# Routing dense edges by half-width column tiles instead of full-width blocks

## The reference

```
h   = relu(layernorm(x))
msg = relu([h[dst], edge_attr] @ W1a + b1a) @ W1b + b1b      # per edge
summed, counts = segment_sum(msg, src), segment_sum(1, src)  # per node
agg = summed / max(counts, 1)
out = x + relu([h, agg] @ W2a + b2a) @ W2b + b2b
```

## Time and profile before

| | |
|---|---|
| median of 2 runs | 1411.84 us (1411.36 to 1412.31) |
| span of the profiled execution, first to last instruction | 1414.2 us |
| mean granted TensorE clock | 0.978 of full speed |
| instructions | 66554, of which TensorE 27554 matmuls and as many weight loads |

### The profile page before, as it was taken

One profiled execution on the slowest core, in us unless ns is written; L12 is line 12 of the kernel. 1 busy time (PEld: TensorE's weight loads), 2 busy tenths in 40 slices (PEclk: granted clock), 3 DMA queues, 4 the chain that ended last, 5 costly groups with the idle time before them and its releaser, 6 DMA issues. The chain is left out here.

```text
span 1414.2 us, 66554 instructions
## 1 busy us (share of the span) xinstructions
PE 1339.5 (95%) x27554; PEld 1298.9 (92%) x27554; DVE 1341.4 (95%) x4186; ACT 869.4 (61%) x1857; POOL 1106.0 (78%) x732
## 2 busy tenths in 40 slices
PE   4667999999999999999999999999999999999967
PEld 3556999999999999999999999999999999999965
DVE  7889999999999999999999999999999999999886
ACT  6246666666666666666666666666666666666505
POOL 3538888888888888887888878888788887888753
PEclk8779999999999999999999999999999999999988
DMA  4767767767777777776777767776677876777451
GB/s 153 303 145 142 120 116 124 123 116 128 125 123 128 116 124 122 123 128 122 119 121 130 129 112 121 127 128 127 108 122 128 125 134 101 125 126 123 64 154 48
DMA packets 225080, 178.60 MB, mean 126 GB/s; under 512 B 149632, under 2 KB 191742, under 8 KB 223751
## 3 DMA queue, kind: packets, MB, share of 16 engines
q1 hardware_dynamic: 130468, 145.66, 39.7%
q0 software_dynamic: 94304, 28.63, 28.5%
HBM read 140.88 MB, written 33.31 MB: 123 GB/s over the span
## 5 line engine op out<-in xcount | busy, mean ns | idle before, releaser
L651 POOL DMA_INDIRECT sums<-vv,sidx x648 | 1043.8, 1611 | 249.9 <-issue 185.7
L892 ACT ACTIVATE area<-rank_ps 64x392 bf16<-64x392 f32 x1150 | 563.7, 490 | 138.1 <-PE rank_ps L1589 114.0
L1603 PE MATMUL rank_ps<-area 128*128 128x65 bf16 x17250 | 614.6, 193 | 1.6 <-issue 1.6
L1603 PEld LDWEIGHTS rank_ps<-area 128*128 128x128 bf16 x17250 | 593.8, 98 | 11.0 <-issue 2.0
L1589 PE MATMUL rank_ps<-r_d,oh 128*128 128x196 bf16 x4600 | 497.6, 250 | 13.3 <-DVE oh L1154 5.3
L1589 PEld LDWEIGHTS rank_ps<-r_d,oh 128*128 128x128 bf16 x4600 | 381.5, 97 | 27.1 <-issue 7.7
L1169 DVE TENSOR_SCALAR area<-iota,local 128x640 bf16<-128x640 int16 x1150 | 397.4, 410 | 4.1
L1154 DVE TENSOR_SCALAR oh<-iota,rank 128x640 bf16<-128x640 int16 x920 | 312.3, 409 | 4.8 <-PE rank_ps L1589 3.7
L869 ACT ACTIVATE r_d<-z_ps 128x512 f32<-128x512 f32 x247 | 147.5, 597 | 81.5 <-PE z_ps L1559 77.9
L880 ACT ACTIVATE vv<-c_ps 128x396 f32<-128x396 f32 x108 | 54.1, 501 | 175.7 <-PE c_ps L1578 165.2
L1553 PE MATMUL z_ps<-wts,et_d 128*128 128x128 f32 x920 | 131.9, 287 | 1.1 <-ACT r_d L869 0.7
(11 more groups left out here) (203 smaller groups left out, 794.8 us busy)
## 6 DMA issues: line engine op xcount, KB each, us to landing
ids_s<-ids SPq DMA_DIRECT2D x216, 192.0 KB
et_d<-in_e_t SPq DMA_DIRECT2D x115, 256.0 KB
ids_d<-ids SPq DMA_DIRECT2D x115, 256.0 KB
et_s<-in_e_t SPq DMA_DIRECT2D x108, 192.0 KB
sums<-vv,sidx POOLq DMA_INDIRECT x648
sums<-dense POOLq DMA_DIRECT2D x4, 1657.5 KB
wp_s<-p_table SPq DMA_DIRECT2D x216, 15.8 KB
wp_d<-p_table SPq DMA_DIRECT2D x115, 15.8 KB
```

The lines of the kernel that those rows point to most:

```text
L651: nc.gpsimd.indirect_dma_start(out=sums[t][:, :], out_offset=bass.IndirectOffsetOnAxis(ap=index, axis=0), in_=rows, in_offset=None, comput ...
L892: ins = nc.scalar.activation(routed[on, t.div(MACRO).mod(2), first:second + 1:second - first, t.mod(MACRO), :], bank[on, :, :], ACT.Copy)
L1603: ins = nc.tensor.matmul(l2_ps[h][:, u * W:u * W + w], oh2[:, g, u * P:(u + 1) * P], rows[:, PARTS[r]:PARTS[r] + w], start=g % MACRO == 0 ...
```

## The change

A routing matmul now takes weights that are 64 wide: the places of one bucket alone. For each bucket the four tiles of the first side write the lower 64 partitions of the bank, and the four tiles of the other side the upper 64, by turns. A fill is two buckets, and a bank holds both halves of each, so one activation copies it whole. The swap of buckets on the second side, and with it five of GpSimd's six operations on `place`, is gone. The branch that doesn't run here gets an index per half, a transfer and some small operations more. Other hunks rename a constant.

```diff
-FILLS = (((0, 0), (0, 1)), ((0, 2), (0, 3)), ((1, 0), (0, 4)), ((1, 1), (1, 2)), ((1, 3), (1, 4)))
+FILLS = tuple((b, b + 1) for b in range(0, BUCKETS, 2))
...
-                halfway = [slice(k * SUB * DENSE, (k + 1) * SUB * DENSE) for k in range(SIDES)]
-                nc.gpsimd.tensor_scalar(place[:, halfway[1]], bucket_b[:, halfway[1]], 0.5, -0.25, ALU.mult, ALU.add).then_inc(place_step, 1)
...
+                nc.gpsimd.tensor_scalar(place, bucket_b, float(PLACES), 1.0, ALU.mult, ALU.add).then_inc(place_step, 1)
...
                         bank = l1_ps[f % 2][:, 0:2 * RW].rearrange("p (i c) -> p i c", c=RW)
+                        first, last = FILLS[f]
                         if fit:
-                            for half in range(SIDES):
-                                first, second = (bucket_at(side, block, half) for side, block in FILLS[f])
-                                on = slice(half * PLACES, (half + 1) * PLACES)
-                                ins = nc.scalar.activation(
-                                    routed[on, t.div(MACRO).mod(2), first:second + 1:second - first, t.mod(MACRO), :], bank[on, :, :], ACT.Copy)
-                            ins.then_inc(routed_ready, 1)
+                            nc.scalar.activation(routed[:, t.div(MACRO).mod(2), first:last + 1, t.mod(MACRO), :], bank,
+                                                 ACT.Copy).then_inc(routed_ready, 1)
                             return
...
-                    for i, (side, block) in enumerate(FILLS[f]):
-                        for k in range(side * SUB, (side + 1) * SUB):
-                            ins = nc.tensor.matmul(l1_ps[f % 2][:, i * RW:(i + 1) * RW], oh1[:, k, block * P:(block + 1) * P],
-                                                   halves(DN, t)[:, k, :], start=k == side * SUB, stop=k == (side + 1) * SUB - 1)
+                    for i, bucket in enumerate(FILLS[f]):
+                        for k in range(SUB):
+                            for side in range(SIDES):
+                                strip = slice(side * PLACES, (side + 1) * PLACES)
+                                ins = nc.tensor.matmul(l1_ps[f % 2][strip, i * RW:(i + 1) * RW],
+                                                       oh1[:, side * SUB + k, bucket * PLACES:(bucket + 1) * PLACES],
+                                                       halves(DN, t)[:, side * SUB + k, :], start=k == 0, stop=k == SUB - 1)
                     ins.then_inc(routing, 1)
```

More of the change, by code:

```diff
@@ L22 @@
 ROWE = GE[DN] + GE[S]
-ROWG = 1 + SIDES
+WINDOWS_S = 2
+ROWG = 1 + WINDOWS_S
 BUCKETS = 10
@@ L104, in done @@
     return n + START
-def bucket_at(side, block, half):
-    return 2 * block + (half ^ side)
 def cols(m, n):
@@ L147, in cycles, with gnn_kernel @@
         s = s.plus(n)
-def gnn_kernel(nc, x, e_t, e_rows, src_col, dst_col, src_row, dst_row, weights, row_biases, out):
+def gnn_kernel(nc, x, e_t, e_rows, src_col, dst_col, src_strips, src_row, dst_row, weights, row_biases, out):
     f32, i32, i16, bf16 = mybir.dt.float32, mybir.dt.int32, mybir.dt.int16, mybir.dt.bfloat16
@@ L280, in gnn_kernel @@
         src_td = spare[:, TILES[DN] * RW + GE[DN] // 2:TILES[DN] * RW + GE[DN] // 2 + DT]
-        assert TILES[DN] * RW + GE[DN] // 2 + DT <= NTP * D and COLS <= 5 * 2 * HALF
+        strip_limit = spare[:, TILES[DN] * RW + GE[DN] // 2 + DT:TILES[DN] * RW + GE[DN] // 2 + DT + STRIPS]
+        assert TILES[DN] * RW + GE[DN] // 2 + DT + STRIPS <= NTP * D and COLS <= 5 * 2 * HALF
         near = rank[:, 0:(2 * ROWS_S + ROWS_D) * 3 * D // 2].bitcast(bf16).rearrange("p (k c d) -> p k c d", c=3, d=D)
@@ L765, in cycle @@
                         if routes:
-                            pool.wait_ge(dsidx_ready, done(t.value(1)))
-                            scatter_any(DN, landed(s.base + n, routed_groups), dsidx[:], lambda k: dsame[:, k, 0:W])
+                            pool.wait_ge(dsidx_ready, done(t.times(STRIPS, STRIPS)))
+                            for strip in range(STRIPS):
+                                scatter_any(DN, landed(s.base + n, routed_groups) + strip * TILES[DN] // ANY_TABLES, dsidx[:, strip, :],
+                                            lambda k: dsame[:, k, 0:W])
                             for at in range(ANY_TABLES):
@@ L887, in keep_routed @@
                         bank = l1_ps[f % 2][:, 0:2 * RW].rearrange("p (i c) -> p i c", c=RW)
+                        first, last = FILLS[f]
                         if fit:
-                            for half in range(SIDES):
-                                first, second = (bucket_at(side, block, half) for side, block in FILLS[f])
-                                on = slice(half * PLACES, (half + 1) * PLACES)
-                                ins = nc.scalar.activation(
-                                    routed[on, t.div(MACRO).mod(2), first:second + 1:second - first, t.mod(MACRO), :], bank[on, :, :], ACT.Copy)
-                            ins.then_inc(routed_ready, 1)
+                            nc.scalar.activation(routed[:, t.div(MACRO).mod(2), first:last + 1, t.mod(MACRO), :], bank,
+                                                 ACT.Copy).then_inc(routed_ready, 1)
                             return
-                        tiles = [side * SUB + block for side, block in FILLS[f] if block < SUB]
                         if f == 0:
                             act.wait_ge(dense_ended, done(t.value()))
-                        if not tiles:
+                        if last >= TILES[DN]:
                             act.wait_ge(routed_ready, done(t.times(len(FILLS), f)))
@@ L902, in keep_routed @@
                             return
-                        nc.scalar.activation(dsame[:, tiles[0]:tiles[-1] + 1, :], bank[:, 0:len(tiles), :], ACT.Copy).then_inc(routed_ready, 1)
+                        nc.scalar.activation(dsame[:, first:last + 1, :], bank, ACT.Copy).then_inc(routed_ready, 1)
                     def cycle(s, n, t, routes, sums_too):
@@ L1366, in dense_rows @@
                             dve.wait_ge(dsum_ready, done(t.times(2, r)))
[L1367 to L1371, removed]
+                        sources = src_td[:, column_of(DN, t):column_of(DN, t) + TILES[DN]]
+                        for j in range(STRIPS):
+                            nc.vector.scalar_tensor_tensor(out=dpick[:, j::STRIPS], in0=dsame[:, j::STRIPS, W],
+                                                           scalar=strip_limit[:, j:j + 1], in1=sources[:, j::STRIPS], op0=ALU.is_lt,
+                                                           op1=ALU.mult).then_inc(dpick_ready, 1)
+                        dve.wait_ge(dpick_ready, done(t.times(STRIPS, STRIPS)))
+                        for strip in range(STRIPS):
+                            on = slice(strip * PLACES, (strip + 1) * PLACES)
+                            nc.vector.tensor_scalar(dsidx[on, strip, :], dpick[on, :], trash[on, 0:1], None, ALU.add).then_inc(dsidx_ready, 1)
                     def cycle(s, n, t, routes, sums_too):
@@ L1408, in general @@
                     dve.wait_ge(ptab_out, 16 * len(P_PARTS))
-                    step(nc.vector.tensor_scalar(src_td, srcf[:, 0:DT], untrash[:, 0:1], None, ALU.add))
+                    dve.wait_ge(dst_in, 32)
+                    step(nc.vector.tensor_scalar(src_td, src_td.bitcast(i32), untrash[:, 0:1], None, ALU.add))
+                    for strip in range(STRIPS):
+                        on = slice(strip * PLACES, (strip + 1) * PLACES)
+                        for j in range(STRIPS):
+                            step(nc.vector.tensor_scalar(strip_limit[on, j:j + 1], limit[on, 0:1], 2.0 ** (PLACES * (strip - j)), None,
+                                                         ALU.mult))
                     step(nc.vector.memset(basew[:], -1.0))
                     step(nc.vector.memset(oh1[:], 0.0))
-                    dve.wait_ge(place_step, 6)
+                    step(nc.vector.memset(dpick[:], 0.0))
+                    for strip in range(STRIPS):
+                        step(nc.vector.tensor_scalar(dsidx[:, strip, :], dpick[:], trash[:, 0:1], None, ALU.add))
+                    dve.wait_ge(place_step, 1)
                     step(nc.vector.memset(words(0, n_routed + n_oh2), 0.0))
@@ L1527, in _ @@
                         pe.wait_ge(ranks_kept, b - 1)
-                    for side, bank in enumerate((l2_ps[b % 2], l1_ps[b % 2])):
-                        mine = masks[:, b, side * SUB:(side + 1) * SUB, :]
-                        ranks = bank[:, 0:SUB * DENSE].rearrange("p (k g) -> p k g", k=SUB)
+                    for half, bank in enumerate((l2_ps[b % 2], l1_ps[b % 2])):
+                        mine = masks[:, b, half * HALF_TILES:(half + 1) * HALF_TILES, :]
+                        ranks = bank[:, 0:HALF_TILES * DENSE].rearrange("p (k g) -> p k g", k=HALF_TILES)
                         for r in range(TURNS):
@@ L1536, in _ @@
                         for before in range(1, SUB):
```

(6 more changed lines are left out.)

36 lines of the change are left out of this document (14 added, 22 removed).

## The result

The changed kernel takes 1533.48 us (two runs, 1532.85 to 1534.11) against 1411.84 before: 1.0866 times as long, 95% interval 1.0835 to 1.0898, or 121.6 us more. The forecast was 1515 us, +104.

What follows compares the result with a forecast made beforehand. TensorE was taken to bound the kernel. Copies, routing pairs, weight loads and GpSimd's place step at 0 and changes of width at +104 us, added to the median of 1411.84, gave 1515 us; range 1404 to 1703, with 82% in it.

Steps and rivals of the forecast that it cites:

- The bound: Main loop: TensorE leads, VectorE has 2.1% of slack, ScalarE 35%; ScalarE follows and its saved copy work is worth nothing.
- Pairs: Routing on TensorE: two 64-wide matmuls run side by side at 87.5 ns, as one full-width matmul did; cost 0.
- Rival 2: Routing pairs: the halves run one after the other, +402 us and somewhat more with the changes, from 1814 us; chance 14%.
- Weight loads: Routing on TensorE: two 64-wide loads take at most 60.6 ns, hidden under the pair's 87.5 ns; cost 0.
- The 104 us kept for them: Routing weight loads falling back to the fp32 pace: 22.5 ns more a pair over 4600 pairs, kept for the range.
- Changes of width: TensorE entering and leaving half-width routing blocks: 1150 changes at 0.09 us, +104 us; bounds 0 and 187 us.
- Rival 1: TensorE routing: pairs side by side, loads hidden, changes free; 1404 to 1420 us, centre 1412; chance 32%.
- Rival 3: Block edges on TensorE: each change waits the whole recorded tail, 1599 us, or 1703 with loads at fp32 pace; chance 12%.
- Rival 4: Routing pairs: half-width matmuls stream quicker, a pair under 81.4 ns, over 2% faster, down to 1378 us; chance 4%.
- ScalarE's 8 us: TensorE's waits for ScalarE's copies, 1.7 + 6.0 us, mostly in the first five cycles: bound -8 us, taken as 0.

Runs made afterwards that it cites:

- the two copying experiments: Kernel before with one 128-partition copy per bank in place of two of 64: 1411.92 us; changed kernel with two 64-partition copies per bank: 1533.36 us.
- one strip: Changed kernel with the matmuls of both sides writing the lower 64 partitions, the upper ones left out: 1921.96 us, one run.
- The small matmuls in the kernel before: Kernel before with one extra 16-column matmul between the two accumulations of every fill: half-width 1537.25 us, full-width 1425.80 us.
- the joined kernel above: Kernel before with fp32 matmuls of the next scattered and next dense group issued next to each other, bf16 ones behind: 1407.80 us, ratio 0.9966.

## Why the prediction was right

- **The bound.** TensorE leads, ScalarE is off the path: shown by the two copying experiments, 1.0007 and no difference.
- **Pairs.** Taken at 87.5 ns with the halves side by side; measured 88.8 ns, and in one strip twice that. The speedup that the Trainium skill's "TensorE: Matmul & The Clock Gate", "Measured speedup vs the span model", gives for column tiles agrees in kind: two tiles took hardly longer here than one full-width matmul. Rival 2, the halves in turn, is the one-strip kernel at 1922 us.
- **Weight loads.** Taken as hidden: inside a block they are, at 88.8 ns a pair, although a 64-wide load is recorded with 108 ns and a 128-wide one with 97. The 104 us kept for them did not come.
- **Changes of width.** This is the term that carried the forecast, and it was sized a little low. I took 0.09 us for each of 1150 changes from the fp32 block, 104 us. Measured are 0.22 us a block, 0.11 a change, over 1110 changes: 122 us. The small matmuls in the kernel before split it: 0.09 in and 0.10 out. The medians of single records in the changed kernel split it further: from the last sum to the first routing matmul 0.12 us where it was 0.03, from the last routing matmul to the first sum 0.18 where it was 0.087. So the change itself costs 0.09 each way, as taken. The rest is slower first work, which I had no term for: the first pair takes 0.113 us and the later ones 0.087, and the first sums are slower too.
- **Rival 1,** nothing paid, fell with the first timeline. **Rival 3,** the whole recorded tail, asked 0.162 us a change and 1599 us; a change costs two thirds of it. The drain that the Trainium skill states ("TensorEngine Tiling (Array Packing)", "Key Properties") agrees with the trace in kind, as the cost comes at every change and not within a block; the price is 0.11 us here, less than the tail a record shows. That the engine empties itself in that time is the page's account; the runs show the price, where it falls, and that the next weight load waits. They don't tell a drain from another reason why that load isn't made ahead. **Rival 4** needed pairs under 81.4 ns.
- **ScalarE's 8 us** of waits, priced at zero, were worth zero: 1411.92 against 1410.78 beside it.

**Luck in the 0.09.** The price was borrowed from the fp32 block, and in the kernel before that block pays for something else:

```profile
706.63 0.35 PE L1553 MATMUL z_ps<-wts,et_s 128*128 128x128 f32 x1
706.72 0.19 PEld L1553 LDWEIGHTS z_ps<-wts,et_s 128*128 128x128 f32 x1
706.82 0.39 PE L1553 MATMUL z_ps<-wts,et_s 128*128 128x128 f32 x2
```

Its first matmul comes on time; the second starts 0.19 us after it in place of 0.11, as its load starts only at 706.72. Leaving the block costs nothing: in the joined kernel above, the eight matmuls at its end take 0.89 us, 0.11 each. By that row half-width work would have paid on the way in alone, 575 x 0.09 = 52 us. That it pays both ways was assumed, and it held. Nothing in the records ties the two prices together; that they are equal was luck.

## What to carry to other kernels

Where two widths of weights alternate on TensorE, count the alternations, not the matmuls: each cost 0.11 us here, which is more than a matmul of 196 columns. Column tiles cost next to nothing inside a block, so a longer block loses less: five blocks a cycle cost 122 us, three 76 and one 51, of which 19 are the pauses for the copies. No run here shows them to gain. And taking work off an engine that already waits is no gain, whatever its busy time shrinks by. To see such a cost, measure start to start over a known count, as the busy line stays full.

## What the runs showed of the hardware that was not expected

One half-width matmul of 16 columns amid full-width work costs some 0.22 us (1537.25 less the 1411.16 of the kernel before beside it, 126 us over 575), nearly nine times the same matmul at full width (14.6 us over 575, 25 ns). In the changed kernel the wait ahead of half-width work is 0.09 us after matmuls of 64 and of 512 columns alike (0.12 us from start to start in place of 0.03, 0.32 in place of 0.23), and ahead of full-width work as much after 196. Four tiles of 32 columns run side by side as well as two of 64 (0.83 against 0.82 us a fill), but the kernel as a whole took 50 us more than the changed kernel, more than half of it in waits to which the profile gives no releaser.
